# Mixture-of-experts stages: x gathered with each row and added to the first choice's result inside the tile loop

## The reference, cut to what matters

```python
x = x + L0_ffn(layernorm(x))      # stage f0: each token goes to one expert of 8, no biases
x = x + L1_xattn(...)             # a1
x = x + L1_ffn(layernorm(x))      # stage f1: two experts of 8, biases b1 and b2
...
x = x + L3_ffn(layernorm(x))      # stage f3: two experts of 8, biases; the last stage, x is the output

# each of the three, for a token t with experts e1 (and e2) and gates g1 (and g2)
y[t] = g1 * (act(xn[t] @ W1[e1] + b1[e1]) @ W2[e1] + b2[e1])  (+ g2 * the same with e2)
```

## Time and profile before

| | |
|---|---|
| median of 3 runs | 1637.09 us (1629.89 to 1640.44) |
| profiled execution | 1637.9 us, its span 1636.2 us |
| busy | PE 1169.2 us (71%), PEld 902.2 (55%), DVE 858.3 (52%), ACT 595.2 (36%), POOL 809.9 (49%) |
| granted TensorE clock over the span | 0.87 of full speed |
| DMA | 96.49 MB in 87405 packets |

### The profile page before, as it was taken

One profiled execution on the slowest core, in us unless ns is written; L12 is line 12 of the kernel. 1 busy time (PEld: TensorE's weight loads), 2 busy tenths in 40 slices (PEclk: granted clock), 3 DMA queues, 4 the chain that ended last, 5 costly groups with the idle time before them and its releaser, 6 DMA issues. The chain is left out here.

```text
span 1636.2 us, 28939 instructions
## 1 busy us (share of the span) xinstructions
PE 1169.2 (71%) x8627; PEld 902.2 (55%) x8627; DVE 858.3 (52%) x2357; ACT 595.2 (36%) x1144; POOL 809.9 (49%) x913
## 2 busy tenths in 40 slices
PE   3448844892776777726776889896999784787773
PEld 2437742781565676615443555553888544676762
DVE  4551136467844444478784553336899526343444
ACT  2124325341344444424321223224445541444441
POOL 6226656464245565542534767863444101566553
PEclk9659987996789899968987999997999995989897
DMA  3041126000511111120304444531000013111115
GB/s 110 2 167 43 47 79 112 1 0 3 173 31 38 42 41 42 41 106 11 97 1 105 98 79 104 115 53 52 1 0 0 8 47 134 40 42 43 39 43 173
DMA packets 87405, 96.49 MB, mean 59 GB/s; under 512 B 19509, under 2 KB 66742, under 8 KB 86774
## 3 DMA queue, kind: packets, MB, share of 16 engines
q1 hardware_dynamic: 63542, 53.61, 11.2%
q0 software_dynamic: 22848, 32.85, 9.1%
q10 hardware_dynamic: 896, 8.55, 1.3%
HBM read 65.71 MB, written 29.26 MB: 58 GB/s over the span
## 5 line engine op out<-in xcount | busy, mean ns | idle before, releaser
L1105 PE MATMUL psum<-f_xsT,f_w1e 128*128 128x128 f32 x1448 | 227.3, 306 | 93.8 <-ACT f_w1e L1140 66.0
L1073 POOL DMA_INDIRECT d_y<-f_y,f_dst x181 | 178.3, 985 | 185.3 <-DVE f_y L1217 148.7
L1105 PEld LDWEIGHTS psum<-f_xsT,f_w1e 128*128 128x128 f32 x1448 | 200.2, 214 | 114.5 <-ACT f_w1e L1140 73.2
L1069 POOL DMA_INDIRECT f_xs<-d_xn,f_src x181 | 175.3, 969 | 140.4 <-POOLq L851 86.2
L1113 PE MATMUL psum<-f_w,f_hT 128*128 x1448 | 213.5, 294 | 4.4 <-ACT f_hT L1155 3.0
L1113 PEld LDWEIGHTS psum<-f_w,f_hT 128*128 128x128 f32 x1448 | 190.2, 205 | 10.9 <-issue 6.2
L1186 DVE TENSOR_TENSOR f_hpre<-psum,f_b 128x512 f32<-128x512 f32 x142 | 98.1, 691 | 181.9 <-issue 68.3
L560 PE MATMUL psum<-ident,xn 128*128 128x128 f32 x256 | 48.3, 366 | 142.9 <-DVE xn L533 142.7
L1155 ACT ACTIVATE f_hT<-f_hpre 128x512 f32<-128x512 f32 x142 | 89.4, 630 | 135.6 <-DVE f_hpre L1186 97.5
L1140 ACT COPY f_w1e<-f_w 128x512 f32 x181 | 111.8, 618 | 54.8 <-PEq L851 48.6
L2422 POOL DMA_INDIRECT d_acc<-f_y,f_token x64 | 100.9, 1576 | 47.8 <-DVE f_y L2750 30.2
(11 more groups left out here) (464 smaller groups left out, 2407.6 us busy)
## 6 DMA issues: line engine op xcount, KB each, us to landing
f_w<-d_y SPq DMA_DIRECT2D x20, 512.0 KB, 7.6
d_xn<-xn ACTq DMA_DIRECT2D x3, 2080.0 KB, 11.7
f_w<-in_L_ffn_W SPq DMA_DIRECT2D x2, 2048.0 KB, 8.7
a_v<-in_ctx SPq DMA_DIRECT2D x4, 1024.0 KB, 7.9
f_wg<-in_WgT SPq DMA_DIRECT2D x16, 256.0 KB
f_wu<-in_WuT SPq DMA_DIRECT2D x16, 256.0 KB
f_wd<-in_WdT SPq DMA_DIRECT2D x16, 256.0 KB
f_xs<-d_xn,f_src POOLq DMA_INDIRECT x181
```

The source lines that it names most:

```text
L1069: nc.gpsimd.indirect_dma_start(xs[:, u % RX, :], None, k.d_xn, bass.IndirectOffsetOnAxis(m.src[:, n:n + 1], 0)).then_inc(gathered[u % RX], 16)
L1073: nc.gpsimd.indirect_dma_start(k.d_y, bass.IndirectOffsetOnAxis(m.dst[:, n:n + 1], 0), y[:, u % RT, :], None).then_inc(scattered[u % RT], 16)
L1105: last = nc.tensor.matmul(BH[u % 2][:, s * P:(s + 1) * P], w1e[:, u % RT, s * P:(s + 1) * P], xsT[:, u % RT, :], start=True, stop=True)
```

## The change

The rows of d_xn grow from 520 B to 1032 B (DROW = GROW + D): behind xn and the gates each row now holds x. `route` writes it with one more DMA on SP, between the loads of w1 and w2, and makes m.first beside m.second. In the loop ScalarE copies the x part of each gathered row aside (keep_x, in f1 and f3 times m.first, so that it is zero for second choices), and DVE makes y as gate × result + kept x in one instruction. GpSimd's gather now also waits until x of the buffer's old tile is kept, and DVE's y until x of its tile is kept. At the end f0 reads its results back right into k.x and adds nothing; f1 and f3 add the two choices once, on DVE. GpSimd adds nothing.

```diff
--- before.py
+++ after.py
@@ -29,6 +29,7 @@
 YROWS = 2 * T + 80 * P
 XROW = 144
 GROW = D + 2
+DROW = GROW + D
 
 
 class Kernel:
@@ -101,8 +102,9 @@
                 js = slice(c * TPC, (c + 1) * TPC)
                 sp.dma_start(k.x[:, js, :], rows[:, js, :]).then_inc(loaded[c], 16)
             sp.wait_ge(filled, 1)
-            sp.dma_start(k.d_xn[T:T + P, :], k.zeros[:, 0:GROW]).then_inc(padded, 16)
-            sp.wait_ge(padded, 16)
+            sp.dma_start(k.d_xn[T:T + P, 0:GROW], k.zeros[:, 0:GROW]).then_inc(padded, 16)
+            sp.dma_start(k.d_xn[T:T + P, GROW:], k.zeros[:, 0:D]).then_inc(padded, 16)
+            sp.wait_ge(padded, 32)
 
         @block.scalar
         def _(act):
@@ -815,7 +817,7 @@
     GR = 8
     NOTOKEN = (127 + 7) * P
     lg = m.lg
-    m.second = sb("second", [P, m.cols])
+    m.second, m.first = sb("second", [P, m.cols]), sb("first", [P, m.cols])
     m.src = sb("src", [P, m.cols], I32)
     m.dst = sb("dst", [P, m.cols], I32)
     m.expert = sb("expert", [1, m.cols], I32)
@@ -852,9 +854,12 @@
             @block.sync
             def _(sp):
 
-                for dst, src in weights:
+                (dst, src), *rest = weights
+                sp.dma_start(dst, src).then_inc(wl, 16)
+                sp.dma_start(k.d_xn[0:T, GROW:].rearrange("(p j) d -> p j d", p=P), k.x[:]).then_inc(xst, 16)
+                for dst, src in rest:
                     sp.dma_start(dst, src).then_inc(wl, 16)
-                sp.wait_ge(xst, 16)
+                sp.wait_ge(xst, 32)
                 sp.wait_ge(wl, 16 * len(weights))
 
             @block.vector
@@ -939,6 +944,7 @@
                 step(TS(tile_i[:], ti[:], 7, None, ALU.arith_shift_right))
                 step(TS(ti[:], tile_i[:], NT - 1, None, ALU.bitwise_and))
                 step(TS(m.second[:], tile_i[:], float(NT), None, ALU.is_ge))
+                step(TS(m.first[:], tile_i[:], float(NT), None, ALU.is_lt))
                 step(nc.vector.scalar_tensor_tensor(out=pp[:], in0=part_i[:], scalar=float(2 * NT), in1=tile_i[:], op0=ALU.mult, op1=ALU.add))
                 step(TT(jj[:], padrow[:], f1[:], ALU.mult))
                 step(TT(m.dst[:], jj[:], pp[:], ALU.add))
@@ -964,7 +970,7 @@
                 act.wait_ge(steps, count_any(m))
                 nc.scalar.activation(gate[:, 1, :], mx[:, 3, :], ACT.Exp).then_inc(exd, 1)
                 act.wait_ge(gates_made, 1)
-                act.dma_start(k.d_xn[0:T, :].rearrange("(p j) d -> p j d", p=P), k.xn_rows[:]).then_inc(xst, 16)
+                act.dma_start(k.d_xn[0:T, 0:GROW].rearrange("(p j) d -> p j d", p=P), k.xn_rows[:]).then_inc(xst, 16)
                 if beside is not None:
                     beside.scalar_rest(act)
 
@@ -1000,14 +1006,15 @@
 
     nc, tag = k.nc, m.tag
     N = m.tiles
-    RX, RT, AHEAD = 4, 4, 6
+    RX, RT, RK, AHEAD = 4, 4, 8, 6
     I = m.cols // RX
     LAST = N - (I - 1) * RX
     BT, BH, BY = (k.bank[0], k.bank[1]), (k.bank[2], k.bank[3]), (k.bank[4], k.bank[5])
     with ExitStack() as st:
         def sb(name, shape, dt=F32):
             return st.enter_context(nc.sbuf_tensor(f"{tag}_{name}", shape, dt))
-        xs = sb("xs", [P, RX, GROW])
+        xs = sb("xs", [P, RX, DROW])
+        x_kept = sb("x_kept", [P, RK, D])
         slot_gate = sb("slot_gate", [P, RX])
         xsT = sb("xsT", [P, RT, P])
         w1e = sb("w1e", [P, RT, FF])
@@ -1017,13 +1024,13 @@
         y_sum = sb("y_sum", [P, RT, D]) if m.b2 is not None else None
         gathered = [k.sem(f"{tag}_gathered{u}") for u in range(RX)]
         scattered = [k.sem(f"{tag}_scattered{u}") for u in range(RT)]
-        x_turned, x_copied, w_copied, up, biased, activated, down, y_ready, gate_kept, y_summed = [k.sem(f"{tag}_{s}") for s in (
-            "x_turned", "x_copied", "w_copied", "up_done", "biased", "activated", "down_done", "y_ready", "gate_kept", "y_summed")]
+        x_turned, x_copied, w_copied, up, biased, activated, down, y_ready, gate_kept, y_summed, kept = [k.sem(f"{tag}_{s}") for s in (
+            "x_turned", "x_copied", "w_copied", "up_done", "biased", "activated", "down_done", "y_ready", "gate_kept", "y_summed", "x_kept")]
         up_read = activated if m.b1 is None else biased
         PARTS, TP = 4, NT // 4
         back = [[k.sem(f"{tag}_y_back{c}{q}") for q in range(PARTS)] for c in range(m.choices)]
-        second, whole, pool_added, stored = [k.sem(f"{tag}_{s}") for s in ("second_added", "first_added", "first_added_by_pool", "out_stored")]
-        results = [w[:].rearrange("p (j d) -> p j d", j=NT) for w in (m.w1, m.w2)]
+        added, stored = [k.sem(f"{tag}_{s}") for s in ("results_added", "out_stored")]
+        results = [w[:].rearrange("p (j d) -> p j d", j=NT) for w in (m.w1, m.w2)] if m.choices == 2 else [k.x]
 
         def tiles(q):
             return slice(q * TP, (q + 1) * TP)
@@ -1038,15 +1045,6 @@
 
             return n < N
 
-        def add(eng, c, q):
-
-            wait(eng, back[c][q], 16)
-            sum_ = flat(k.x[:, tiles(q), :])
-            return eng.tensor_tensor(sum_, flat(results[c][:, tiles(q), :]), sum_, ALU.add)
-
-        def wait_whole(eng, q):
-
-            eng.wait_ge((whole, pool_added)[q % 2], q // 2 + 1)
         with nc.Block() as block:
             @block.sync
             def _(sp):
@@ -1059,7 +1057,7 @@
                         sp.dma_start(results[c][:, tiles(q), :], rows[:, c, tiles(q), :]).then_inc(back[c][q], 16)
                 if out is not None:
                     for q in range(PARTS):
-                        wait_whole(sp, q)
+                        sp.wait_ge(added, q + 1)
                         sp.dma_start(out[:, tiles(q), :], k.x[:, tiles(q), :]).then_inc(stored, 16)
                     sp.wait_ge(stored, 16 * PARTS)
 
@@ -1075,17 +1073,15 @@
                 for n in range(AHEAD):
                     wait(pool, x_turned, n - RX + 1)
                     wait(pool, gate_kept, n - RX + 1)
+                    wait(pool, kept, n - RX + 1)
                     gather(n, n)
                 for n in range(N):
                     if n + AHEAD < N:
                         wait(pool, gate_kept, n + AHEAD - RX + 1)
+                        wait(pool, kept, n + AHEAD - RX + 1)
                         gather(n + AHEAD, n + AHEAD)
                     pool.wait_ge(y_ready, n + 1)
                     scatter(n, n)
-                for q in range(1, PARTS, 2):
-                    if m.choices == 2:
-                        pool.wait_ge(second, q + 1)
-                    add(nc.gpsimd, 0, q).then_inc(pool_added, 1)
 
             @block.tensor
             def _(pe):
@@ -1144,6 +1140,16 @@
                     wait(act, up, n - RT + 1)
                     nc.scalar.copy(xsT[:, u % RT, :], BT[u % 2][:, 0:P]).then_inc(x_copied, 1)
 
+                def keep_x(n, u):
+
+                    act.wait_ge(x_turned, n + 1)
+                    wait(act, y_ready, n - RK + 1)
+                    row, at = xs[:, u % RX, GROW:], x_kept[:, n % RK, :]
+                    if m.choices == 1:
+                        nc.scalar.copy(at, row).then_inc(kept, 1)
+                    else:
+                        nc.scalar.activation(at, row, ACT.Copy, scale=m.first[:, n:n + 1]).then_inc(kept, 1)
+
                 def activate(n, u):
                     wait(act, down, n - RT + 1)
                     if m.b1 is None:
@@ -1162,17 +1168,22 @@
                         if exists(n + 2):
                             activate(n + 2, u + 2)
                         if exists(n + 4):
+                            keep_x(n + 4, u + 4)
                             copy_w(n + 4, u + 4)
                 copy_w(0, 0)
                 copy_x(0, 0)
+                keep_x(0, 0)
                 copy_w(1, 1)
                 copy_x(1, 1)
+                keep_x(1, 1)
                 activate(0, 0)
                 copy_w(2, 2)
                 copy_x(2, 2)
+                keep_x(2, 2)
                 activate(1, 1)
                 copy_w(3, 3)
                 copy_x(3, 3)
+                keep_x(3, 3)
                 groups(body)
 
             @block.vector
@@ -1214,7 +1225,9 @@
                             dve.wait_ge(y_summed, n + 1)
                             src = y_sum[:, u % RT, :]
                         dve.wait_ge(gate_kept, n + 1)
-                        nc.vector.tensor_scalar(y[:, u % RT, :], src, slot_gate[:, u:u + 1], None, ALU.mult).then_inc(y_ready, 1)
+                        dve.wait_ge(kept, n + 1)
+                        nc.vector.scalar_tensor_tensor(out=y[:, u % RT, :], in0=src, scalar=slot_gate[:, u:u + 1], in1=x_kept[:, n % RK, :],
+                                                       op0=ALU.mult, op1=ALU.add).then_inc(y_ready, 1)
                 for n in range(3):
                     keep_gate(n, n)
                 if m.b1 is not None:
@@ -1223,20 +1236,22 @@
                 groups(body)
 
                 def measure(q):
-                    wait_whole(dve, q)
```

(21 more changed lines are left out.)

## The result

The kernel after takes 1659.34 us (median of 4 runs, 1658.13 to 1661.43); the kernel before took 1634.8 beside it (1629.89 to 1640.44). The ratio is 1.015, 95% interval 1.011 to 1.019: slower, by 1.5%. The forecast was 1658 us. The time was met, but not by the steps that led to it. To see that, take the four kinds of stretch apart, in the profiled executions (spans 1636.2 and 1656.5 us).

The account below looks back on a forecast made before the run. The tile loop was seen as a ring with little slack, GpSimd's two indirect DMAs setting a tile's minimum. 1637.9 + 11.4 (routing) − 8.3 (ends) + 18 (loops) = 1659.0, against the median 1658 us; range 1641 to 1683.

Parts of the forecast that it names:

- the choice of the rate: Routing: x's store priced at 0.28 MB/us, from a store into rows 576 B apart, so 7.5 us.
- pieces that start off any boundary at half of the row's rate, +16 us: Routing of f0: upper end of the stores' cost, +16 us where +8.0 was forecast.
- rival C: Whole kernel: stores near half rate, more loop waits passed on, TensorE's clock lower; 1683 us, chance 0.2.
- The cover of 1.9 us: Routing of f0: weights land 1.9 us before DVE's chain ends, so that much added transfer time would hide.
- the later turn of b1: Routing of f1: weights come late, TensorE waits some 3.1 us to turn b1, all reaching the loop: +3.1.
- f3's slack behind DVE: Routing of f3: b1 at 1373.3 is late for its turn but not for DVE's copy at 1375.69: 0.
- the price of keep_x's place: Loops, ScalarE: keep_x delays the copy of w1 by 0.54 us a tile, 22 of 37 passed on: +12 us.
- +2 for y: Loops, DVE: y as scalar_tensor_tensor takes 344 ns against 290, +0.05 a tile: +2 us, bounds 0 and 8.
- +4 for the gathers: Loops: wider gathers land 0.22 us later, a quarter of 74 TensorE waits pass it on: +4, bounds 0 and 16.
- Rival A: Loops: the later copy of w1 falls into slack, loops cost +3; total 1644 us, chance 0.2.
- −6.8, −1 and −0.5: Ends of f0, f1, f3: GpSimd's additions and DRAIN stop holding f0 and f1, f3's last store goes sooner; −8.3 together.
- The slower case, at 0.62: Whole kernel: measured time more than about 1% above before, beyond 1621 to 1653 us; chance 0.62.

Follow-up runs that it names:

- e5: The changed kernel with rows padded to 1088 B, so that every piece starts on a multiple of 64 B: 1639.14 us, ratio 1.002 to before.
- e6: The changed kernel with rows padded to 1088 B (pieces on 64 B) and x stored in the layer norm ahead of the routing: 1627.67 us, ratio 0.996.
- e2: The changed kernel with x stored before the routing, in the layer norm ahead of it, rows not padded: 1519.20 us, ratio 1.001.
- after again: The changed kernel run once more, unaltered, for its profile on another chip: 1657.76 us, ratio 1.012.
- before again: The kernel before run once more, unaltered, for its profile on that same chip: 1632.70 us, ratio 0.999.
- e8: The kernel before with f0's two GpSimd additions at the end made by DVE instead: 1514.17 us, ratio 1.000.
- e9: Against e6, x rides with f0's rows only; f1 and f3 keep 576 B rows, loop and ends of the kernel before: 1513.93 us, ratio 0.998.
- e11: The same kernel as e6, run once more on another chip: 1517.72 us, ratio 0.999.
- e1: The changed kernel with both stores to d_xn on SP's queue, x first, then xn: 1558.51 us, ratio 1.027.
- e3: The changed kernel with keep_x moved ahead of the activation on ScalarE: 1549.92 us, ratio 1.021.

## Why the prediction was right, and where it wasn't

**Routing: the step that failed is the choice of the rate.** "0.28 MB/us, so 7.5 us for x" took the row of a store of equal size, and the bounds named the right case, "pieces that start off any boundary at half of the row's rate, +16 us", for f0, without taking it. That case happened: 0.17 MB/us, +13.3 in f0, +10.7 in f1 (above its bound of 8) and +6.7 in f3 (where 0 was said for the stores). Even rival C had no more than 20 us for the three, and 30.7 were measured. What made the row the wrong one could be read off it: its pieces start every 576 B, those of the change every 1032. e5 is the check of everything else in the step: with pieces on 64 B, and so at the row's rate, the routings grow by 6.9, 3.1 and 0.2 us, where the sum had 8.0, 3.2 and 0.2. The cover of 1.9 us, the later turn of b1, and f3's slack behind DVE were sized well, and only the rate was off.

The rate is also where the Trainium skill was weighed. Its page "DMA: Bandwidth & Descriptors" (Specifications) names 512 B as the least for line rate. Read as enough, as the prediction read it, the traces go further against it than the row did: pieces of 512 B run at 290 GB/s (e6) or at 170 (e2). "Collectives: The Full Stack" (Rules for kernel authors) asks for buffers aligned to 32 B to prevent a read-modify-write. It says so of collectives; the runs here agree in so far as pieces on 64 B are fast, but no run tried 32 B, and none shows that the mechanism is that one.

**Loops: the price of keep_x's place was over-sized.** "Only then can the load begin" was wrong together with the 0.65 us behind it: the copy starts 0.29 us after keep_x does. The delay is 0.18 us a tile and not 0.54, and TensorE's waits for the copy grew neither in number (37) nor in sum (73.2 to 65.5 us). By itself 0.18 us in 22 of 37 passes is 4 us instead of 12, and the whole of the loops, by the profiles, +4.5 instead of +18. Two more comparisons of profiles say +8.0 (after again against before again) and +6.5 (e5). The other two terms, +2 for y and +4 for the gathers, weren't measured apart; TensorE's waits for landings, without the first tiles, grew by 4.6 us. Rival A, "the loop swallows it" (+3), came nearest on the loops; its total of 1644 failed by the routing. That 1658 was met is luck: with the measured routing and loops the sum, 1637.9 + 30.7 − 8.3 + 4.5, makes 1665, 7 above the profiled execution, and f2's 8 us close that gap.

**Ends: right.** −6.8, −1.7 and −0.3 us stand against −6.8, −1 and −0.5, and e8 shows for f0 that the reason was the right one: the DRAIN of GpSimd behind its addition. In f1 the last addition and the statistics behind it take 4.3 us in the kernel after; 4.5 was worked out.

**Unchanged code.** f2 took 8.0 us less after than before. In the second pair of profiles it took 347.6 and 347.1 us. So nothing ties the 8 us to the change; they are how far two executions of one stage can differ, and a time for a stage of 350 us from one profile has that uncertainty.

**The bound "within 1%" and the chances.** The slower case, at 0.62, came. It came by the routing alone, where the forecast had meant the loop to carry most of it; rival C's first part (stores near half rate) happened without its other two, and no drop of the granted clock came with them: 0.91 in f3's loop of the kernel after against 0.89.

## What to carry to other kernels

When rows of a DRAM tensor are widened, look at where each piece starts, not only at how long it is: one pad of 56 B in each row, which puts both pieces on multiples of 64 B, took the stores from 170 to 290 GB/s and 18 us out of this kernel. A price taken from a row of the same kernel is good only if that row shares what matters, here pitch and start. And a total that comes out right says nothing of its terms: compare stretch by stretch, with one unchanged stage beside them as a measure of chance.

## What was unexpected of the hardware

**A slow store starts fast.** The pieces that start off 64 B run at 289 GB/s for the first 2 us, and only then at 170 (e2, nothing beside them). By these numbers a transfer of half a megabyte would not show the loss. Nor is every piece slow: in e2 they take 29 ns on average in the first 2 us and 57 behind them, where 28% take over 60 ns, one 816, and 43% still 35 or less. In e6 no piece of x takes more than 54 ns. The reason stays open.

**Chips 7% apart, and a kind of stop that only one has.** The kernel before takes 1634 us on the chip of call 2 and 1518 on those of calls 1 and 3, and the loops make nearly all of it: of the 116 us between the spans of before again and e8 (whose loops are the kernel's before), the three loops have 104; f1's takes 233.6 us in the one and 192.4 in the other. On the chip of call 2, and in the main measurement, the waits list stops that no other engine explains ("remote"); in the eight executions of calls 1 and 3 there is none. GpSimd's wait for y, 148.7 us in the earlier trace rows, is small there (e8, whole span):

```profile
POOL d_y L1073 <- DVE f_y L1217: 26.6, 17, 5.6
```

What these stops are stays unknown, and that they make the whole difference isn't shown.

**Less clock in a longer loop.** In e9's f3 loop (190.2 us) TensorE is granted the full clock (2.4 GHz) in every stretch of 20 us but the first; in e11's, with the wide gather and keep_x, at 205.0 us, it isn't. Two stretches of each, first e9, then e11:

```profile
1333.00:1353.00 20.00, 18.42 (x135) 16.01 (x135) 11.09 (x32) 11.49 (x24) 15.23 (x16) 1.00 0.19 55
1393.00:1413.00 20.00, 18.39 (x128) 15.35 (x128) 10.96 (x31) 11.38 (x23) 15.43 (x16) 1.00 0.20 58
```

```profile
1337.00:1357.00 20.00, 16.60 (x118) 15.14 (x119) 9.46 (x27) 10.68 (x28) 13.22 (x14) 0.91 0.24 73
1397.00:1417.00 20.00, 16.79 (x123) 15.53 (x122) 11.03 (x31) 11.67 (x29) 13.60 (x14) 0.91 0.25 73
```

TensorE is busy for 16.7 us of 20 in those two, against 18.4, and gets less clock (0.91 is a mean over a stretch in which it fell to its lower level, 1.2 GHz, for part of the time). Over the whole loops it is 0.94 in e11 and 0.98 in e9. Whether the waits lowered the clock or the lower clock lengthened the work isn't shown, and one stretch of e11 with 15.6 us busy had the full clock. It isn't the change that lowers it, since e1, e2 and e3, with the same gather and keep_x, have 0.96 to 0.98 in this loop. Loops of one kernel can lie more than 10 us apart, so the price of a small wait in them can't be read from a single execution.
